# Mixture-of-experts stage of a Trainium2 kernel: gathers four slots ahead, and a second product whose distance shrinks from seven slots to two

## The chip, the cores and the metric

One NeuronCore of a Trainium2 chip. The metric is the device time of one execution in microseconds (us). The profile describes one execution, with the times of each instruction and transfer.

## What is computed

The input x has 4 sequences of 1024 tokens with 512 features. It is normalized by row (xn), and the output is the sum of three terms: x, causal attention with 16 heads and ALiBi biases on xn, and a mixture of 8 experts on xn, of which each token uses the best 2:

```
topw, sel = top_k(softmax(xn @ gate_w.T), 2); topw = topw / sum(topw)
gate_up = einsum('th,eoh->eto', xn, w1)          # 8 experts, 2*352 columns
g, u = split(gate_up, 2)
act = silu(g) * u
expert_out = einsum('eti,ehi->eth', act, w2)
out = einsum('eth,te->th', expert_out, combine)  # combine holds topw at sel
```

## The kernel before, in words

One function, `plan`, writes out the whole order of the work as a list of steps; each engine's function (`sync`, `tensor`, `vector`, `scalar`, `gpsimd`) walks through this one list and emits the steps that are its own, so the order within each engine is the order of the list. Steps of different engines meet through semaphores.

The first part (about 1180 us) computes normalization, attention, the routing and the split of the expert weights into pairs of fp16 numbers, which go to HBM and are read back at its end. Each normalized token row is kept in HBM as 1024 fp16 numbers (`xn_d`). The routing sorts the 8192 token-expert pairs by expert into NSLOT = 71 slots of 128 rows (`tl` holds the token numbers and weights of each slot). The output array already holds x plus attention when the experts begin.

The expert stage is one loop over slots. For a slot s the steps are:

- `gather` (POOL, L1664): an indirect DMA brings the 128 token rows of slot s (256 KB) into `xg`. There are XDEEP buffers; it waits for the transposition `mxt` of slot s - XDEEP.
- `mxt` (SP, L903): a transposing DMA from `xg` to `xT`, also XDEEP buffers. It waits for the gather of s and for the first product of slot s - XDEEP.
- `mgu` (PE, L1060): the first product, 24 matmuls into one of two PSUM buffers S (printed as "S").
- `msig`, `mglu`, `mah`, `mal` (ACT L1561, DVE L1434 and L1435, ACT L1569, DVE L1441): the gated activation, split in two fp16 parts.
- `mat`, `mac` (PE L1075, DVE L1449 and L1450): its six transpositions through PSUM (T) into `aTm`, which has AHEAD + 1 = 8 buffers.
- `mdn` (PE, L1091): the second product, 9 matmuls into PSUM O or M, in turn.
- `myo` (ACT, L1576): copies it, scaled by the row's weight, to `yo` in SBUF. Two buffers: it waits for the scatter of slot s - 2.
- `scatter` (POOL, L1675): an indirect DMA adds the 128 rows (256 KB) to the output in HBM. Different slots may hold the same token, so each scatter waits until the one before has landed.

In the loop (see `plan`) iteration s issues gather(s+2) and mxt(s+2), mgu(s), the transposition of slot s-1, the activation of slot s, and then mdn, myo and scatter of slot s-7 (AHEAD = 7). So on POOL's queue gather(s+2) stands right behind scatter(s-8), and on PE mdn(s-7) stands behind mgu(s). After the last first product, seven slots still have their second product and scatter to come. The semaphore waits of POOL's own list keep this order: a gather behind a waiting scatter waits too.

Of the kernel before, what the change touches and what calls it, by code (L numbers as in the profile page):

```python
# [8 lines left out]
P = 128  # L9
B, S, E = 4, 1024, 512  # L10
# [21 lines left out]
LAG = 4  # L32
J_ORDER = [0, 7, 1, 6, 2, 5, 3, 4]
AHEAD = 7
XDEEP = 3
ARENA = 50240
SLOPES = [2.0 ** (-0.5 * (h + 1)) for h in range(H)]
PASS = [(0, 0), (0, 1), (1, 0)]
# [97 lines left out]
def plan():  # L136
# [432 lines left out]
    def gather(s):  # L569
        add("gather", s, sem=f"xg{s % XDEEP}", inc=16)  # L570

# [14 lines left out]
    def turn_a(s):  # L586
# [2 lines left out]
        add("mac", s)  # L589
        o.leave("T", ("mat", s), ("mac", s))  # L590

    def down(s):
        o.take("Y", "mdn", s)
        add("mdn", s)
        add("myo", s)
        o.leave("Y", ("mdn", s), ("myo", s))
        add("scatter", s, inc=16)

    add("experts", inc=0)
    for s in range(XDEEP - 1):  # L600
        gather(s)
        turn_x(s)
    for s in range(NSLOT + AHEAD):
        if s + XDEEP - 1 < NSLOT:
            gather(s + XDEEP - 1)
            turn_x(s + XDEEP - 1)
        if s < NSLOT:
            up(s)
        if 1 <= s <= NSLOT:
            turn_a(s - 1)  # L610
        if s < NSLOT:
            gated(s)
        if s >= AHEAD:
            down(s - AHEAD)
    return o


# [18 lines left out]
def build(nc, ctx, T):  # L636
# [15 lines left out]
    def at(*step):  # L652

        name, value = o.count[step]
        return sems[name], value
# [84 lines left out]
    ac, to = place(to, [P, 2, I], F32)  # L740
    ah, to = place(to, [P, 2, 2, I], F16)
    aTm, to = place(to, [P, AHEAD + 1, 6, P], F16)
    yo, to = place(to, [P, 2, E], F32)
    assert to <= LATE, to

    GU = [ps(f"S{i}", [P, 1024], F32) for i in range(2)]
    SBK = [GU[0], GU[1][:, 0:512]]
# [705 lines left out]
    def scalar(act):  # L1453
# [4 lines left out]
        for step in o.steps:  # L1458
# [8 lines left out]
            elif kind == "xnd" and not key[0]:  # L1467
                b, half, i = key
                t = b * 8 + half * 4 + i
                on.wait_ge(*at("xnl", *key))  # L1470
                act.dma_start(xn_d[t * P:(t + 1) * P, :], XH[half_place(*key)]).then_inc(at(*step)[0], 16)
            elif kind == "xt" and key[3] == "a":
                b, half, i, _ = key
                tt = half * 4 + i
                tz = MBK[o.bank["xtp", b, half, i]][:, :].bitcast(F16)
                on.wait_ge(*at("xtp", b, half, i))
                if b:
                    on.wait_ge(*at("v", b - 1, NG - 1, 1, 3))
                act.activation(xnT[:, :, :, tt * P:(tt + 1) * P].rearrange("p a c n -> p (a c) n"),
                               tz.rearrange("p (c n) -> p c n", c=8), ACT.Copy).then_inc(sems["xta"], 1)  # L1480
            elif kind == "wqh":
                c, = key
                on.wait_ge(sems[f"w{c}"], 16)
                on.wait_ge(*at("scales", 0))
                act.activation(wqkv[:, 0, c, :], rawW[:, c, :], ACT.Copy, scale=col(SW)).then_inc(sems["wqh"], 1)
            elif kind == "gwh":
                on.wait_ge(sems["bias"], 32)
                on.wait_ge(*at("scales", 1))
                act.activation(gwh[:, 0, :, :].rearrange("p c n -> p (c n)"), gwf[:, :, :].rearrange("p c n -> p (c n)"),
                               ACT.Copy, scale=col(SG)).then_inc(sems["gwh"], 1)  # L1490
            elif kind == "woh":
                on.wait_ge(sems["w4"], 16)
                on.wait_ge(*at("scales", 2))
                act.activation(wo[:, 0, :, :].rearrange("p c n -> p (c n)"), rawA[:, 6144:8192], ACT.Copy,
                               scale=col(SWO)).then_inc(sems["woh"], 1)
            elif kind == "qk32":
                b, g, qk, half = key
                if (b, g, qk, half) != (0, 0, 0, 0):
                    n = 4 * (b * NG + g) + 2 * half + qk - 1
                    on.wait_ge(sems["qkl"], n + 1)  # L1500
                on.wait_ge(*at("qk", *key, 2))
                on.wait_ge(*at("scales", 1))
                cs, bs = (cq[:, g:g + 1], bq[:, g:g + 1]) if qk == 0 else (col(CK), bk[:, g:g + 1])
                act.activation(t32[:, 0, :], MBK[o.bank["qk", b, g, qk, half]][:, :], ACT.Identity, bias=bs,
                               scale=cs).then_inc(sems["qk32"], 1)
            elif kind == "exp":
                u, = key
                b, g, j, h, k, par = unit(u)
                w, r, m = P * (j + 1), u % 4, u % 8
                on.wait_ge(*at("mx", u))  # L1510
                if u >= 16:
                    on.wait_ge(*at("rx", u // 8 * 8 - 9))
                c = 4 * (1 - u % 2) + h
                act.activation(ring[r][:, 0:w], ring[r][:, 0:w], ACT.Exp, bias=mneg[:, m:m + 1], scale=-1.0,  # L1514
                               accum_out=rs[:, k, c:c + 1]).then_inc(sems["exp"], 1)
            elif kind == "pt" and key[2] == "a":
                u, i, _ = key
                k, h = unit(u)[4], unit(u)[3]
                c0, c1, to_, gap = turn_parts(u)[i]
                n = (c1 - c0) * P  # L1520
                on.wait_ge(*at("tr", u, i))
                if u >= 16:
                    on.wait_ge(*at("pv", u // 8 * 8 - 9))
                act.activation(PT[:, k, h, to_:to_ + gap * (c1 - c0 - 1) + 1:gap, :],  # L1524
                               TB[o.bank["tr", u, i]][:, 0:n].rearrange("p (c n) -> p c n", n=P),
                               ACT.Copy).then_inc(sems["pta"], 1)
            elif kind == "rsb":
                u, = key
                on.wait_ge(*at("rt", u))
                if u >= 8:  # L1530
                    on.wait_ge(*at("a32", u - 8))
                act.activation(Rsb[:, :], OB[:, 2 * P:4 * P], ACT.Copy).then_inc(sems["rsb"], 1)
            elif kind == "wsh":
                i, = key
                n, rows = w_rows(i)
                s = col(S1) if WCHUNK[i][1] < 4 else col(S2)
                on.wait_ge(*at("wload", "split", i))
                on.wait_ge(*at("wscale", 4))
                if i:
                    on.wait_ge(*at("wstore", i - 1))  # L1540
                else:
                    on.wait_ge(*at("xnd", 0, 1, 3))
                act.activation(hl[0:rows, 0, 0, 0:n], raw[0:rows, o.bank["wload", "split", i], 0:n], ACT.Copy,
                               scale=s[0:rows]).then_inc(sems["wsh"], 1)
            elif kind == "rex":
                on.wait_ge(*at("route", 0))
                act.activation(pr, pr, ACT.Exp).then_inc(sems["rex"], 1)
            elif kind == "experts":
                on.wait_ge(*at("pv", NU - 1))
                on.wait_ge(*at("rt", NU - 1))  # L1550
                on.wait_ge(*at("aT", NU - 1))
                for i in range(8):
                    on.wait_ge(*at("o", B - 1, i, 2))
                on.wait_ge(*at("listr"))
            elif kind == "msig":
                s, = key
                m = s % 2
                on.wait_ge(*at("mgu", s))
                if s >= 2:
                    on.wait_ge(*at("mal", s - 2))  # L1560
                act.activation(ex[:, m, :], GU[o.bank["mgu", s]][:, 0:I], ACT.Sigmoid,  # L1561
                               scale=col(I1)).then_inc(sems["msig"], 1)
            elif kind == "mah":
                s, = key
                m = s % 2
                on.wait_ge(*at("mglu", s))
                if s >= 2:
                    on.wait_ge(*at("mat", s - 2))
                act.activation(ah[:, m, 0, :], ac[:, m, :], ACT.Copy).then_inc(sems["mah"], 1)  # L1569
            elif kind == "myo":  # L1570
                s, = key
                m = s % 2
                on.wait_ge(*at("mdn", s))
                if s >= 2:
                    on.wait_ge(*at("scatter", s - 2))
                act.activation(yo[:, m, :], YB[o.bank["mdn", s]][:, :], ACT.Copy,  # L1576
                               scale=tl[:, s, 1:2].bitcast(F32)).then_inc(sems["myo"], 1)

    def gpsimd(pool):
# [10 lines left out]
        for step in o.steps:  # L1590
# [76 lines left out]
            elif kind == "scatter":  # L1667
# [4 lines left out]
                else:  # L1672
# [1 line left out]
                        on.wait_ge(*at("ostore", B - 1, i))  # L1674
                pool.indirect_dma_start(  # L1675
                    out=T["out"], out_offset=bass.IndirectOffsetOnAxis(tl[:, s, 0:1].bitcast(U32), 0),
                    in_=yo[:, s % 2, :], in_offset=None, compute_op=ALU.add).then_inc(sems["scatter"], 16)
        on.wait_ge(*at("scatter", NSLOT - 1))

    block = ctx.enter_context(nc.Block())  # L1680
# [74 lines left out]
```

## Time and profile before

| | us |
|---|---|
| median of 3 runs | 1713.99 |
| lowest, highest | 1702.82, 1714.74 |
| profiled execution, its time | 1701.79 |
| its span, first to last instruction | 1699.8 |

In the rows below times are us from the start of the span. PE is the matmul engine, PEld its weight loads, DVE, ACT and POOL the vector, scalar and GpSimd engines, SP the engine that issues most plain DMAs. "[1.67 <-X]" at the end of a timeline row is the engine's idle time just before it and what ended it. "issue" is time in which the engine waited for nothing that the profile shows. A DMA's "landing" is counted from the start of the instruction that issued it.

### The profile page before, as it was taken

The numbers are of one execution on the slowest core, as the hardware profiler recorded it, in microseconds if no ns is written. First come the engines' busy times: TensorE is split into PE (matmuls) and PEld (weight loads), VectorE is DVE, ScalarE is ACT, GpSimd is POOL, SyncE is SP. The second block draws the span as 40 slices with busy tenths as digits, with TensorE's granted clock in tenths as the row PEclk, the third lists the DMA queues.
The fourth block names the chain that finished last, engine by engine and source line by source line (L and its number), as shares of the span: only waits on it lengthen the run. The fifth ranks groups of instructions, "written<-read, shape, count | busy, mean of one in ns | idle before, by whom it ended". The sixth has DMA issues, their size and how long they took to land.

```text
span 1699.8 us, 35183 instructions
## 1 busy us (share of the span) xinstructions
PE 1472.6 (87%) x12629; PEld 875.3 (51%) x12629; DVE 1031.1 (61%) x2450; ACT 886.3 (52%) x2027; POOL 492.3 (29%) x576
## 2 busy tenths in 40 slices
PE   1699998998998899999899999995899998999882
PEld 1365564555555555555555555552555555555541
DVE  5478787675788777787788777772433333333320
ACT  3177776664777666776765577771222222222220
POOL 3111133121113212113311566411143343434322
PEclk9899999998999999999999999998899999999996
DMA  6153531333333254453133422545466666666653
GB/s 242 24 144 105 145 95 49 102 102 101 111 96 100 77 148 139 130 145 88 50 91 105 120 74 79 196 162 216 111 112 121 117 120 123 120 124 117 126 82 43
DMA packets 163460, 193.40 MB, mean 114 GB/s; under 512 B 88480, under 2 KB 104096, under 8 KB 163168
## 3 DMA queue, kind: packets, MB, share of 16 engines
q1 hardware_dynamic: 143760, 151.22, 32.3%
q0 software_dynamic: 17952, 37.30, 12.0%
q8 instruction: 109, 1.79, 0.4%
q10 hardware_dynamic: 1584, 2.64, 0.4%
q14 instruction: 55, 0.45, 0.1%
HBM read 93.45 MB, written 53.88 MB: 87 GB/s over the span
## 4 chain that ended last, share of the span: by engine, by line
PE 47%; DMA 16%; DVE 12%; issue 11%; ACT 6%; SPq 4%; POOL 3%; DVEq 0%; ACTq 0%; POOLq 0%
PE T L992 10%; PE S L1060 7%; PE O L1008 7%; DMA out<-arena,tl 6%; PE S L981 5%; PE M L949 4%; DMA arena<-arena 4%; PE S L949 4%; DMA arena<-xn_d,tl 4%; SPq L841 3%; DVE arena L1347 3%; PE M L1031 2%; ACT arena L1514 2%; ACT arena L1524 2%; PE S L966 2%
## 5 line engine op out<-in xcount | busy, mean ns | idle before, releaser
L1347 DVE CUSTOM_DVE_ANT_0 arena<-S,cF,nsl 128x1024 f32<-128x1024 f32 (+7 forms) x512 | 413.4, 811 | 58.5 <-PE S L981 54.5
L992 PE MATMUL T<-cF,arena 128*128 128x128 f32 x2304 | 366.9, 280 | 71.2 <-ACT arena L1524 37.4
L1514 ACT ACTIVATE arena<-arena,mneg 128x1024 f32<-128x1024 f32 (+7 forms) x512 | 395.3, 772 | 47.7 <-DVE mneg L1347 46.8
L1524 ACT ACTIVATE arena<-T 128x512 f32<-128x512 f32 (+3 forms) x543 | 241.6, 458 | 247.2 <-PE T L992 243.1
L992 PEld LDWEIGHTS T<-cF,arena 128*128 128x128 f32 x2304 | 266.8, 142 | 173.0 <-ACT arena L1524 44.6
L1060 PE MATMUL S<-arena 128*128 x1704 | 274.0, 319 | 59.4 <-issue 30.6
L1060 PEld LDWEIGHTS S<-arena 128*128 128x128 f16 x1704 | 168.6, 99 | 167.1 <-issue 77.4
L1358 DVE COPY arena<-T 128x512 f32<-128x512 f32 (+3 forms) x289 | 153.8, 535 | 130.2 <-PE T L992 128.4
L1008 PE MATMUL O<-arena 128*32 128x128 f32 (+1 forms) x3328 | 210.9, 329 | 9.0 <-DVE arena L1378 7.7
L981 PE MATMUL S<-arena 96*128 96x512 f16 (+3 forms) x768 | 211.9, 330 | 4.6 <-DVE mneg L1347 3.0
L1675 POOL DMA_INDIRECT out<-arena,tl x71 | 111.9, 1577 | 281.0 <-ACT arena L1576 194.7
L1449 DVE COPY arena<-T 128x512 f16<-128x512 f16 x71 | 30.1, 424 | 249.7 <-PE T L1075 249.7
L1561 ACT ACTIVATE arena<-S,sc 128x352 f32<-128x352 f32 x71 | 39.3, 553 | 227.5 <-PE S L1060 227.5
L1621 POOL TENSOR_TENSOR arena<-arena 128x512 f16<-128x512 f32 x64 | 74.2, 1159 | 271.8 <-DVE arena L1328 264.7
L1008 PEld LDWEIGHTS O<-arena 128*32 128x32 f32 x3328 | 67.3, 109 | 130.0 <-issue 114.0
L1631 POOL CAST arena<-arena 128x256 f16<-128x256 f32 x64 | 27.4, 428 | 308.8 <-DVE arena L1378 308.8
L949 PE MATMUL M<-arena 128*128 128x512 f16 x384 | 99.3, 387 | 14.6 <-DVE arena L1272 14.6
L1514 ACT ACTIVATION_READ_ACCUMULATOR arena<-arena,mneg 128x1 f32 x512 | 99.9, 195 | 0.0
L949 PE MATMUL S<-arena 128*128 128x512 f16 x384 | 99.0, 386 | 0.0
L1569 ACT ACTIVATE arena<-arena 128x352 f16<-128x352 f32 x71 | 35.2, 496 | 110.4 <-DVE arena L1435 110.4
L1664 POOL DMA_INDIRECT arena<-xn_d,tl x71 | 69.8, 983 | 62.7 <-DMA arena<-arena 41.3
L1638 POOL TENSOR_TENSOR arena<-arena 128x512 f32<-128x512 f32 x32 | 40.4, 1275 | 162.3 <-DMA arena<-in_x 162.3
(168 smaller groups left out, 1810.1 us busy)
## 6 DMA issues: line engine op xcount, KB each, us to landing
arena<-arena SPq DMA_DIRECT2D x192, 128.0 KB, 2.4
arena<-in_w1T SPq DMA_DIRECT2D x64, 352.0 KB
arena<-in_x SPq DMA_DIRECT2D x64, 256.0 KB, 3.6
w_d<-arena SPq DMA_DIRECT2D x32, 352.0 KB
arena<-w_d SPq DMA_DIRECT2D x16, 704.0 KB, 10.1
arena<-in_w2T SPq DMA_DIRECT2D x32, 256.0 KB
out<-arena SPq DMA_DIRECT2D x32, 256.0 KB, 2.2
xn_d<-arena SPq DMA_DIRECT2D x24, 256.0 KB, 2.0
```

Source lines behind the costliest of these rows:

```text
L949: tp = pe.matmul(z[:, :], wqkv[:, w_, c, f:f + P], xnT[:, a, c, half * 512:half * 512 + 512], start=(third == 0 and c == 0), stop=(third = ...
L981: tp = pe.matmul(z[:, n0:n1], stk[par][0:96, h, 0, j * P:(j + 1) * P], stk[par][0:96, h, 1, n0:n1], start=True, stop=True)
L992: tp = pe.transpose(z[:, (c - c0) * P:(c - c0 + 1) * P], ring[u % 4][:, c * P:(c + 1) * P], idf)
L1008: tp = pe.matmul(OB[32 * x:32 * x + 32, f:f + n], V[par][:, kt, x * D:(x + 1) * D], flat[:, x, c * P:c * P + n], start=(kt == 0), stop=(kt ...
L1060: tp = pe.matmul(y[:, i * 512:i * 512 + I], xT[:, s % XDEEP, 4 * a + c, :], weights[:, bass.ds(reg[s] + (w_ * NX * W1N + c * 2 * I + i * I ...
L1347: dve.tensor_tensor_reduce(ring[r][:, 0:w], SBK[o.bank["score", u]][:, 0:w], rel[:, S - w:S], nsl[:, hh:hh + 1], 3.0e38, ALU.add, ALU.min, ...
L1358: dve.tensor_copy(PT[:, k, h, to_:to_ + gap * (c1_ - c0_ - 1) + 1:gap, :], TB[o.bank["tr", u, i]][:, 0:n].rearrange("p (c n) -> p c n", n= ...
L1514: act.activation(ring[r][:, 0:w], ring[r][:, 0:w], ACT.Exp, bias=mneg[:, m:m + 1], scale=-1.0, accum_out=rs[:, k, c:c + 1]).then_inc(sems[ ...
L1524: act.activation(PT[:, k, h, to_:to_ + gap * (c1 - c0 - 1) + 1:gap, :], TB[o.bank["tr", u, i]][:, 0:n].rearrange("p (c n) -> p c n", n=P), ...
L1621: pool.tensor_tensor(st[:, 2 * qk + 1, lo:hi], t32[:, 0, :], st[:, 2 * qk, lo:hi], ALU.subtract).then_inc(sems["qkl"], 1)
L1664: pool.indirect_dma_start(out=xg[:, s % XDEEP, :], out_offset=None, in_=xn_d, in_offset=bass.IndirectOffsetOnAxis(tl[:, s, 0:1].bitcast(U3 ...
L1675: pool.indirect_dma_start(out=T["out"], out_offset=bass.IndirectOffsetOnAxis(tl[:, s, 0:1].bitcast(U32), 0), in_=yo[:, s % 2, :], in_offse ...
```

## The change

XDEEP becomes 4: gathers are issued four slots ahead and token transpositions three slots ahead, each with four buffers. YDEEP = 4 gives `yo` four buffers instead of two; it now lies where the weights of the attention's output projection were. The distance between mgu and mdn is a function of the slot: 7 up to s = 24, then one less every 11 slots (6 from s = 25, 5 from 36, 4 from 47, 3 from 58, 2 from 69). Where it gets smaller, one iteration carries two second products with their scatters.

```diff
-XDEEP = 3
+XDEEP = 4
+YDEEP = 4
@@
+    done = [0]
+    def behind(s):
+        return max(2, AHEAD - max(0, s - 14) // 11)
@@
     add("experts", inc=0)
+    for s in range(XDEEP):
+        gather(s)
     for s in range(XDEEP - 1):
-        gather(s)
         turn_x(s)
     for s in range(NSLOT + AHEAD):
+        if s + XDEEP < NSLOT:
+            gather(s + XDEEP)
         if s + XDEEP - 1 < NSLOT:
-            gather(s + XDEEP - 1)
             turn_x(s + XDEEP - 1)
         if s < NSLOT:
             up(s)
@@
-        if s >= AHEAD:
-            down(s - AHEAD)
+        while done[0] <= min(s - behind(s), NSLOT - 1):
+            down(done[0])
+            done[0] += 1
@@
-    yo, to = place(to, [P, 2, E], F32)
-    assert to <= LATE, to
+    assert to <= LATE, (to, LATE)
+    yo, to = place(LATE, [P, YDEEP, E], F32)
@@ scalar, myo
-                if s >= 2:
-                    on.wait_ge(*at("scatter", s - 2))
-                act.activation(yo[:, m, :], YB[o.bank["mdn", s]][:, :], ACT.Copy,
+                if s >= YDEEP:
+                    on.wait_ge(*at("scatter", s - YDEEP))
+                act.activation(yo[:, s % YDEEP, :], YB[o.bank["mdn", s]][:, :], ACT.Copy,
@@ gpsimd, scatter
-                    in_=yo[:, s % 2, :], in_offset=None, compute_op=ALU.add).then_inc(sems["scatter"], 16)
+                    in_=yo[:, s % YDEEP, :], in_offset=None, compute_op=ALU.add).then_inc(sems["scatter"], 16)
```

## Rows read from the trace of the kernel before

**Rows 1.** The page's head: span and busy time by engine

```profile
span 1699.8 us, 35183 instructions
PE 1472.6 (87%) x12629; PEld 875.3 (51%) x12629; DVE 1031.1 (61%) x2450; ACT 886.3 (52%) x2027; POOL 492.3 (29%) x576
```

**Rows 2.** Busy time by stretch: us, engines, clock, DMA share, GB/s

```profile
1200.00:1250.00 50.00, 48.26 (x339) 30.72 (x337) 23.49 (x53) 14.63 (x27) 11.54 (x10) 1.00 0.50 98
1232.00:1636.00 404.00, 369.40 (x2395) 218.97 (x2393) 135.85 (x306) 99.67 (x184) 157.66 (x123) 0.99 0.67 119
1643.00:1700.00 57.00, 25.49 (x104) 10.84 (x102) 2.84 (x7) 6.43 (x10) 12.43 (x8) 0.71 0.33 42
```

**Rows 3.** Timeline of PE in the expert stage: start, us, engine, line

```profile
1235.16 0.50 PE L1075 MATMUL T<-idh,arena 128*128 128x128 f16 x6
1235.49 2.12 PE L1091 MATMUL M<-arena 128*128 x9
1237.45 3.74 PE L1060 MATMUL S<-arena 128*128 x24
1241.03 0.50 PE L1075 MATMUL T<-idh,arena 128*128 128x128 f16 x6
...
1251.15 3.75 PE L1060 MATMUL S<-arena 128*128 x24 [1.67 <-DMA arena<-arena]
```

**Rows 4.** Chain that ended last, 1237 to 1258: start, us, what

```profile
1237.86 0.68 ACT arena L1576
1238.81 1.57 POOL out L1675
1240.68 4.36 DMA arena<-xn_d,tl
1245.06 5.21 DMA arena<-arena
1250.26 0.89 issue
1251.15 3.75 PE S L1060 x24
...
1257.44 0.68 ACT arena L1576
1258.38 1.58 POOL out L1675
```

**Rows 5.** Waits, 1232 to 1636: total us, times, longest

```profile
POOL out L1675 <- ACT arena L1576: 181.7, 47, 12.5
...
POOL out L1675 <- DMA out<-arena,tl: 57.7, 15, 5.0
...
PE S L1060 <- DMA arena<-arena: 26.2, 19, 2.0
```

**Rows 6.** The scatter's line L1675, 1233 to 1636

```profile
L1675 POOL DMA_INDIRECT out<-arena,tl x62: 1569/1583/1637, 1232.8 to 1635.0; - x62
...
DMA to landing us min/median/max: 4.6/5.5/7.0
```

**Rows 7.** The scatter's line L1675, 1650 to 1700

```profile
L1675 POOL DMA_INDIRECT out<-arena,tl x8: 1552/1554/1555, 1651.1 to 1690.6; - x8
...
DMA to landing us min/median/max: 4.7/4.8/5.1
```

**Rows 8.** Timeline of POOL, 1373 to 1387

```profile
1373.16 1.57 POOL L1675 DMA_INDIRECT out<-arena,tl  x1 [4.22 <-DMA out<-arena,tl]
1375.04 0.99 POOL L1664 DMA_INDIRECT arena<-xn_d,tl  x1 [0.30 <-issue]
1379.03 1.58 POOL L1675 DMA_INDIRECT out<-arena,tl  x1 [3.00 <-DMA out<-arena,tl]
1380.92 0.99 POOL L1664 DMA_INDIRECT arena<-xn_d,tl  x1 [0.30 <-issue]
1385.67 1.57 POOL L1675 DMA_INDIRECT out<-arena,tl  x1 [3.77 <-DMA out<-arena,tl]
```

**Rows 9.** The tail's chain: one scatter to the next

```profile
1679.41 4.84 DMA out<-arena,tl
1684.29 0.71 issue
1685.00 4.84 DMA out<-arena,tl
```

More of the change, by code:

```diff
@@ L1571, in scalar @@
                 s, = key
-                m = s % 2
                 on.wait_ge(*at("mdn", s))
-                if s >= 2:
-                    on.wait_ge(*at("scatter", s - 2))
-                act.activation(yo[:, m, :], YB[o.bank["mdn", s]][:, :], ACT.Copy,
+                if s >= YDEEP:
+                    on.wait_ge(*at("scatter", s - YDEEP))
+                act.activation(yo[:, s % YDEEP, :], YB[o.bank["mdn", s]][:, :], ACT.Copy,
                                scale=tl[:, s, 1:2].bitcast(F32)).then_inc(sems["myo"], 1)
```

## The prediction, on record before the changed kernel ran

> **What bounds the kernel now.** The page's head comes first: PE is busy 87% of the span [rows 1], but that is a mean over different stages and the change touches only the last 500 us. So the second view is the busy time by stretch [rows 2]. While first products run without second ones (1200 to 1250, mostly), PE is busy 48.3 of 50 us. From 1232 to 1636, where each iteration has both, it is busy 369.4 of 404 us (91%) at a granted clock of 0.99, and the DMA engines 67%. In the tail, from 1643 on, PE is busy 25.5 of 57 us. The third view is the timeline of PE [rows 3]: an undisturbed iteration takes 1241.03 - 1235.16 = 5.87 us from one activation transposition to the next, and a disturbed one has its first product waiting 1.67 us for a token transposition. There are 19 such waits in the stretch, 26.2 us [rows 5].
>
> The actual pace is read at the scatters: the first starts at 1232.8 and the 62nd at 1635.0 [rows 6], so 402.2 / 61 = 6.59 us per slot, 0.72 more than PE needs. The chain of waits tells why [rows 4]: scatter at 1238.81, gather behind it at 1240.68, landed at 1245.04, transposition landed at 1250.27, first product at 1251.15, then the second product behind it on PE, its copy at 1257.44, the next scatter of the same chain at 1258.38. That is 19.57 us. In slots: scatter(k) is followed on POOL by gather(k+10); after mgu(k+10) PE runs mdn(k+3), which feeds scatter(k+3). So the ring turns three slots in 19.57 us, 6.52 per slot, which is the 6.59 measured. **The bound is the latency of this ring**, not an engine.
>
> Right behind it stands a second bound. Scatters are serial: each waits for the landing of the one before. In the tail, beside no gather or transposition, they land in 4.8 us [rows 7] and follow each other every 5.6 us (4.84 landing plus 0.71 of issue [rows 9]); the eight of them go from 1651.1 to 1690.6, 39.5 / 7 = 5.64 each. Beside the other transfers the median landing is 5.5 us, the longest 7.0 [rows 6]. In 15 of the 62 cases it is already the scatter's own landing that released the next one, and in 47 the copy on ACT [rows 5].
>
> **The change part by part.**
> *Gathers four ahead, transpositions three.* No transfer or instruction is added; 71 gathers and 71 transpositions stay. On POOL, gather(s+4) now stands behind scatter(s-8), so scatter(k) is followed by gather(k+12), and behind mgu(k+12) comes mdn(k+5). The same 19.57 us now carry five slots: 3.9 per slot. The ring is off the path. With the shorter distance it stays so (at distance 2 scatter(k) is followed by gather(k+7), and behind mgu(k+7) again comes mdn(k+5)). The gather's wait on mxt(s) doesn't bind, since mgu(s), just ahead, needs the same; the transposition's wait on mgu(s-1) leaves three iterations of 5.87 us for some 6 us of work (5.21 + 0.89, [rows 4]). At the start one more gather is issued beside the weight loads. I take nothing for it; the bound is below one gather's landing, 4.4 us late, if PE's first product waited for it, and -1 us.
>
> *What is late next.* PE needs 5.87 per slot, the scatter chain its landing plus 0.7. The price of the contended scatter decides everything, and no row shows it in the new regime, so I bound it. Lower end: 5.87, where PE binds, since the scatter alone would do 5.64. Upper end: the periods in which the landing did release the next scatter, 57.7 / 15 = 3.85 us of idle time [rows 5] plus 1.58 scatter, 0.30 and 0.99 gather [rows 6, 8], = 6.72. This is biased upward, since a scatter becomes the bound just when it was slow. The median landing gives 5.5 + 0.7 = 6.2 to 6.25. Where scatters in a row were bound by landing, as at 1373.16, 1379.03 and 1385.67 [rows 8], periods of 5.87 and 6.64 follow each other, mean 6.25; a few landings near 7.0 lift that. The order on the DMA engines in the new regime is the one of these rows (gather 1.9 us behind the scatter, transposition when the gather has landed), so I take 6.35, near the median row rather than the selected one.
>
> *The sum.* Scatter 0 starts as before at 1232.8: distance and first iterations are unchanged. Of the 70 periods to scatter 70, 59 carry a gather (12 to 70) and 11 don't (before: 61 and 9). 59 x 6.35 = 374.7, 11 x 5.64 = 62.0, together 436.7, against 1690.6 - 1232.8 = 457.8 now. After the last scatter's start come 9.2 us in both. The saving is 21.1 us.
>
> *Distance from seven to two.* It moves five second products (about 2 us each, [rows 3]) from behind the last first product to before it. In the kernel before that would shorten the tail of serial scatters, 5.64 each. Here I price it at nothing by itself: the scatters are late against PE anyway, and moving PE's work doesn't move them. The cover is PE's slack: 59 x (6.35 - 5.87) = 28 us against 5 x 2 us of moved work. If that cover were gone (scatters at PE's pace) the moved work would be hidden in part, and the tail shorter by up to 5 x 5.64 = 28 us against what seven pending slots would take.
>
> *Four buffers for the copy.* Before, `myo` waits for scatter(s-2), and behind it on ACT stand the next sigmoid and cast, for which DVE and PE wait in turn. With four it can only wait less. In the stretch ACT's copies are not seen waiting except in the tail, so it is worth 0 to 3 us, and I take 0. With two scatters in one iteration (five times) it keeps the second one's copy from blocking ACT.
>
> A rule to weigh. The trace shows 4.8 us for a lone scatter of 256 KB and 5.5 us beside other traffic [rows 6, 7]. The Trainium skill, page "DMA: Bandwidth & Descriptors", section "Anatomy of one DMA — SWDGE (gpsimd) path", has a fit of about 2.0 us plus bytes / 436e3, which would be 2.6 us here. By that estimate the scatter chain would take about 3.3 us a slot, PE would bind at once, and the kernel would land on the first rival's time. The traces stand against it, even for the lone scatter.
>
> **The rivals.**
> *PE becomes the bound.* If contended scatters come down to 5.1 us of landing or less, the pace is PE's 5.87: 59 x 5.87 + 62.0 = 408.3, 49.5 us saved, 1664.5. For it: after a longer pause scatters land in 4.6 to 5.1, the low end of [rows 6]. Against it: packed closer, they land later. 0.13.
> *No gain.* The scatter chain paces at the selected 6.72: 59 x 6.72 + 62.0 = 458.5, +0.7 us, 1714.7. For it: the 15 waits already there. Against: their selection. 0.15.
> *Slower.* Gathers and transpositions, now free of the ring, lie beside every scatter on the same DMA engines (67% busy already, [rows 2]), and its landing moves to halfway between median and longest, 6.25 us: a period of 7.0, 59 x 7.0 + 62.0 = 475.0, +17.2 us, 1731.2. It decides from a mean period of (457.8 - 62.0) / 59 = 6.71. The ring before left pauses in which a scatter ran alone; without them there are none. Against: the number of bytes and the order are the same. 0.10.
>
> **How the numbers follow.** The forecast case has 0.62. The profiled execution took 1701.8 (its span and 2.0 around it), 12 us less than the median of 1714.0; the three runs are 1702.8, 1714.0 and 1714.7. I apply the saving to the median: 1714.0 - 21.1 = 1692.9 (an execution like the profiled one would come to 1680.7). Its own range is a period of 6.2 to 6.5, 1684 to 1702. A measurement of this kernel can tell about 1% from no change, 17 us, which needs a period below 6.42; of the forecast case I give that 0.7. Faster by over 1%: 0.62 x 0.7 + 0.13 = 0.56. Slower by over 1%: 0.09. Within 1%: 0.35. The range takes in PE's bound below and the no-gain case above: 1664 to 1716.
>
> **What would show it.** Right: PE's waits for token transpositions are not on the path, or are there without cost; nearly all scatters in the middle are released by the landing of the one before (now 15 of 62); 6.2 to 6.5 us between scatters; ACT's copies wait for scatters in the middle too; the first scatter still near 1233; 9 us behind the last scatter's start. Wrong: the scatters are mostly released by ACT's copy (then PE or a ring binds), or the median landing leaves 5.4 to 5.8, or the first product starts late. If the number of scatters behind the last first product falls to three and the tail after it gets shorter by several 5.64 us, the distance was worth more than I give it.

## The result, and the profile after

| | before | changed |
|---|---|---|
| median, us | 1710.97 (4 runs) | 1685.73 (4 runs) |
| lowest, highest | 1702.82, 1714.74 | 1681.75, 1689.71 |
| profiled execution, its time and span | 1701.79, 1699.8 | 1683.42, 1681.5 |

The ratio is 0.9859, with a 95% interval of 0.9811 to 0.9907. A second comparison beside the experiments gave 0.990 (0.9862 to 0.9938). The prediction was 1692.9 against a median of 1714.0, which is a ratio of 0.9877; for an execution like the profiled one it gave 1680.7, and 1683.4 came. The medians moved by 25.2 us and the two profiled executions by 18.4. The four executions of the kernel before spread over 12 us, and only one of them has a trace, so where that spread lies isn't known.

The busy time by stretch and the waits of the changed kernel from 1232 to 1636 answer to [rows 2] and [rows 5]:

```profile
1232.00:1636.00 404.00, 379.83 (x2445) 225.42 (x2444) 136.12 (x308) 103.05 (x189) 162.27 (x123) 0.97 0.67 119
```

```profile
POOL out L1684 <- DMA out<-arena,tl: 186.4, 54, 5.5
POOL out L1684 <- ACT arena L1585: 40.3, 9, 11.4
...
PE S L1070 <- DMA arena<-arena: 16.7, 4, 6.0
...
ACT arena L1585 <- DMA out<-arena,tl: 0.7, 1, 0.7
```

These rows show a bound change hands. Of the 64 scatters that start there, 54 are released by the landing of the one before, where it was 15 of 62; PE's waits for token transpositions fell from 19 (26.2 us) to 4 (16.7 us). The scatter's own line, to set beside [rows 6]:

```profile
L1684 POOL DMA_INDIRECT out<-arena,tl x64: 1562/1569/1827, 1232.7 to 1632.3; - x64
...
DMA to landing us min/median/max: 4.6/5.5/7.2
```

The first scatter stands where it stood, the landing is the same 5.5 us, and 63 periods take 399.6 us, 6.34 each, where 61 took 6.59 each before. In the kernel before, the same 63 periods took 418.3 us (1232.8 to 1651.1), and the last of them was by far the longest, 10.14 us. It is the last turn of the ring, here in the chain that ended last:

```profile
1629.06 1.58 POOL out L1675
...
1630.94 6.34 DMA arena<-xn_d,tl
...
1637.30 3.95 DMA arena<-arena
1641.25 0.97 issue
1642.21 5.43 PE S L1060 x24
...
1651.12 5.06 DMA out<-arena,tl
```

The last gather took 6.34 us to land, and the last first product took 5.43 us at a granted clock of 0.68. In the changed kernel the period at that place is 6.4 us. So some 4 of the 18.3 us that the stage lost come from this one turn.

The timeline of POOL shows the new rhythm, with each scatter here waiting for the last one's landing:

```profile
1461.81 1.57 POOL L1684 DMA_INDIRECT out<-arena,tl  x1 [3.12 <-DMA out<-arena,tl]
1463.68 1.01 POOL L1673 DMA_INDIRECT arena<-xn_d,tl  x1 [0.30 <-issue]
1467.95 1.56 POOL L1684 DMA_INDIRECT out<-arena,tl  x1 [3.25 <-DMA out<-arena,tl]
```

In the expert stage the chain that ended last is now mostly scatters (19% of the whole span, 6% before). Gathers and transpositions, 8% before, are no longer among its larger lines.

```profile
PE 45%; DMA 22%; issue 11%; DVE 11%; ACT 6%; SPq 3%; POOL 2%; POOLq 0%; DVEq 0%; ACTq 0%
DMA out<-arena,tl 19%; PE T L1002 11%; PE O L1018 7%; PE S L991 5%; PE M L959 4%; PE S L959 4%; PE S L1070 4%; DVE arena L1357 3%; SPq L851 3%; PE M L1041 2%; ACT arena L1524 2%; PE S L976 2%; ACT arena L1534 2%; DVE arena L1368 1%; PE M L976 1%
```

### The profile page after: what moved, and what is told of

Its sections match the earlier page's. It is cut to its first block, busy times and chain, and to the rows that moved or that the text cites. A ratio compares the mean times of both kernels' runs of the same rounds, so it can differ in the third digit from the quotient of the medians.

```text
span 1681.5 us, 35180 instructions
## 1 busy us (share of the span) xinstructions
PE 1464.8 (87%) x12629; PEld 874.1 (52%) x12629; DVE 1032.1 (61%) x2450; ACT 886.9 (53%) x2027; POOL 496.0 (29%) x576
## 4 chain that ended last, share of the span: by engine, by line
PE 45%; DMA 22%; issue 11%; DVE 11%; ACT 6%; SPq 3%; POOL 2%; POOLq 0%; DVEq 0%; ACTq 0%
DMA out<-arena,tl 19%; PE T L1002 11%; PE O L1018 7%; PE S L991 5%; PE M L959 4%; PE S L959 4%; PE S L1070 4%; DVE arena L1357 3%; SPq L851 3%; PE M L1041 2%; ACT arena L1524 2%; PE S L976 2%; ACT arena L1534 2%; DVE arena L1368 1%; PE M L976 1%
```

## The experiments

The experiments ran on two chips; whether the first comparison ran on one of them isn't known. In the experiments the kernel before has a median of 1734 to 1739 us. The profiled executions there spend 26 to 32 us more ahead of the experts (the first product starts between 1220 and 1226 in all but one, instead of 1194). So each run is read by its ratio to the kernel before on its own chip, and by its expert stage, here the time from the first to the last scatter's start: 457.8 before, 439.5 changed. The stage is read from one execution of each kernel, and the kernel before was traced only in the first comparison. So a difference of a few us in the stage proves nothing unless the ratio agrees.

**The distance held at seven**

```diff
-        return max(2, AHEAD - max(0, s - 14) // 11)
+        return AHEAD
```

> The change with the distance held at seven throughout (four gathers, four copy buffers stay). Theory (the serial chain of scatters binds, so where PE's second products stand doesn't matter): first scatter near 1233, 70 periods of about 6.28 us as in the changed kernel, span 1678 to 1686, ratio to the kernel before 0.984 to 0.990. Rival (the shorter distance carries part of the gain by moving second products ahead of the last first product): the span is 10 to 20 us longer than the changed kernel's, 1692 to 1702.

Ratio 0.9883 (0.9854 to 0.9912), scatters from 1257.6 to 1698.8, 441.3 us. The theory held: with gathers four ahead, the shorter distance adds nothing that can be measured. It does move work: with distance seven, 11 scatters start behind the start of the last first product, with the shrinking distance 6 (5 when the changed kernel ran again). The stage is as long all the same.

**Distance, or so it was meant**

```diff
-XDEEP = 4
-YDEEP = 4
+XDEEP = 3
+YDEEP = 2
```

> Only the shrinking distance, with three gather buffers, gathers two ahead and two copy buffers as before. Theory (the ring scatter, gather, transposition, first product, second product still binds at 19.6 us for three slots): median period between scatters stays near 6.5 to 6.6, and the shorter tail is paid for by ring pace: ratio to the kernel before 0.997 to 1.004. Rival (distance alone shortens the tail): five scatters of 5.64 us gone from the tail, 15 to 28 us faster, ratio 0.984 to 0.991.

Ratio 0.9865 (0.9827 to 0.9903), stage 434.5 us: the whole gain, and the rival seemed right. But the edit wasn't what the text says. In the changed kernel's loop the gather is XDEEP ahead and the transposition XDEEP - 1; with XDEEP = 3 the gather is three slots ahead, where the kernel before had two. Two later runs take it apart. (The profiled execution, 1706.2 us, is 6 us below this run's median, about as much as its stage is below 440.)

**Two copy buffers**

```diff
-YDEEP = 4
+YDEEP = 2
```

> The change with two buffers for the scaled copy of the second product instead of four. Theory: the scatter chain binds and the copy only has to be ready one scatter ahead: 0 to 3 us more than the changed kernel, ratio to the kernel before 0.984 to 0.990, with copies on ACT now waiting for scatters. Rival (a blocked copy holds the sigmoid and cast behind it on ACT, and so PE, until scatters starve): 8 us or more, ratio over 0.991.

Ratio 0.9879 (0.9849 to 0.9908), stage 439.6 us. The waits of this run from 1232 to 1636:

```profile
POOL out L1684 <- DMA out<-arena,tl: 160.5, 46, 4.8
ACT arena L1585 <- DMA out<-arena,tl: 159.5, 49, 5.9
```

The copies now wait 160 us in all for scatters and it costs nothing that can be measured (0.9883 with four buffers and distance seven, 0.990 for the changed kernel again). This fits the theory: the scatter that they wait for is the one that binds anyway.

**Distance two from the first slot**

```diff
-        return max(2, AHEAD - max(0, s - 14) // 11)
+        return 2
```

> The change with distance two from the first slot. Theory (the serial chain of scatters binds, so the whole stage moves with its first scatter): the first scatter starts near 1213 instead of 1232.7, the 70 periods take 440 to 444 us, span 1662 to 1668, ratio to the kernel before 0.973 to 0.979. Rival (the seven slots are a cushion: without them PE's stalls reach the scatters): periods of 6.5 us and more, span 1675 or longer.

Ratio 0.9767 (0.9733 to 0.9801), median 1696.7 against 1713.7 for distance seven on the same chip: 17 us less. The timelines of PE and POOL in this run:

```profile
1229.59 9.71 PE L1070 MATMUL S<-arena 128*128 x48 [22.43 <-issue]
...
1244.79 0.50 PE L1085 MATMUL T<-idh,arena 128*128 128x128 f16 x6
1245.12 1.68 PE L1101 MATMUL O<-arena 128*128 x7
```

```profile
1248.44 1.64 POOL L1684 DMA_INDIRECT out<-arena,tl  x1 [16.83 <-ACT arena L1585]
```

The first scatter starts 18.9 us behind the first product, 38.5 us in the changed kernel (1194.17, 1232.66). The stage takes 444.0 us from there, and the last scatter starts 462.9 us behind the first product instead of 478.0. The start moved 20 us and the end 15. (This execution began its experts 3 to 10 us later than the others of the experiments, so its absolute times are late.)

**The changed kernel again**

> The changed kernel once more, beside the others on one chip. Ratio to the kernel before as found, 0.981 to 0.991; first to last scatter 437 to 443 us, 6.2 to 6.4 us each while gathers run.

Ratio 0.990 (0.9862 to 0.9938), stage 440.7 us.

**Two chains of scatters**

```diff
-        add("scatter", s, inc=16)
+        add("scatter", s, sem=f"scatter{s % 2}", inc=16)
...
+    out2_d = dram("out2_d", [(NT + 1) * P, E], F32)
...
-                if s:
-                    on.wait_ge(*at("scatter", s - 1))
-                else:
+                if s > 1:
+                    on.wait_ge(*at("scatter", s - 2))
+                elif s == 0:
...
-                    out=T["out"], ...
+                    out=(out2_d if s % 2 else T["out"]), ...
```

> The changed kernel with the scatters of odd slots going to a second array, so that a scatter waits only for the one two before; the second array is left out of the output. Theory (the serial chain of scatters binds): the pace falls to PE's 5.87 us per slot, PE's second product of the last slot ends about 45 us earlier, and the span is 35 to 50 us shorter than the changed kernel's; ratio to the kernel before 0.957 to 0.967, scatters released by the copy on ACT. Rival (the DMA engines as a whole bind, the chain only shows it): landings stretch beyond 7 us and the span falls by less than 15 us, ratio over 0.976.

Ratio 0.9588 (0.9532 to 0.9643). Busy time of this run from 1330 to 1600, and POOL's timeline:

```profile
1330.00:1600.00 270.00, 270.00 (x1780) 162.20 (x1779) 99.60 (x225) 75.60 (x139) 121.02 (x94) 1.00 0.83 136
```

```profile
1400.97 1.57 POOL L1685 DMA_INDIRECT out<-arena,tl  x1 [2.99 <-ACT arena L1586]
1402.85 1.02 POOL L1674 DMA_INDIRECT arena<-xn_d,tl  x1 [0.30 <-issue]
1406.84 1.56 POOL L1685 DMA_INDIRECT out_d<-arena,tl  x1 [2.98 <-ACT arena L1586]
```

The output lacks the sums of the odd slots, since the second array is left out of it. PE is busy 270.00 of 270 us, the pace is its 5.87 per iteration (in each block of 11 iterations the shrinking distance lets 12 scatters through, 5.5 us each), 63 of the 71 scatters are released by ACT's copy and only 3 by a landing, and the stage takes 385.4 us. With the chain split PE is what is left, and the DMA engines are busy 83% without binding. (The rival was to show itself by landings beyond 7 us; the profile gives no landings for this run, but the span fell by 51 us, where the rival allowed less than 15.) So the serial wait is the bound of the changed kernel, and the next one, PE, stands 55 us of stage below it.

**Without gathers, and without transpositions**

```diff
-        if s + XDEEP < NSLOT:
+        if s + XDEEP < 12:
             gather(s + XDEEP)
...
```

```diff
-        if s + XDEEP - 1 < NSLOT:
+        if s + XDEEP - 1 < 12:
             turn_x(s + XDEEP - 1)
...
```

The lines not shown drop or replace the semaphore waits for steps that no longer exist.

> The changed kernel with the gathers of slots 12 to 70 left out (old rows are transposed again). It prices the gather's share of a contended scatter. Theory (a scatter beside other transfers lands later, 5.5 against 4.8 us): median landing 5.0 to 5.2 us, pace 5.87, set by PE, span 22 to 30 us shorter than the changed kernel's, ratio 0.969 to 0.975. Rival (gathers don't disturb scatters, transpositions do): landing stays at 5.4 to 5.5 and the span within 6 us, ratio 0.982 to 0.990.

> The changed kernel with the token transpositions of slots 12 to 70 left out (the first product uses old ones). It prices the transposition's share. Theory: median landing 5.0 to 5.2 us, pace 5.87, span 22 to 30 us shorter than the changed kernel's, ratio 0.969 to 0.975. Rival (transpositions don't disturb scatters, gathers do): landing 5.4 to 5.5, span within 6 us, ratio 0.982 to 0.990.

Ratios 0.971 (0.9648 to 0.9771) and 0.967 (0.9615 to 0.9725). The landing of a scatter from 1330 to 1600, in the changed kernel, without gathers, and without transpositions:

```profile
DMA to landing us min/median/max: 4.7/5.5/7.2
```

```profile
DMA to landing us min/median/max: 4.7/5.0/5.6
```

```profile
DMA to landing us min/median/max: 4.7/4.9/5.8
```

Without the gathers a scatter lands 0.5 us earlier, without the transpositions 0.6, and the stage falls from 440 to 411 and to 401 us. The two don't add up: a scatter beside neither lands in 4.8 [rows 7], so taking one away brings nearly all of it. The first run stayed within its forecast of the ratio. The second gained more than forecast: the ratio was to be 0.969 to 0.975 and the landing 5.0 to 5.2. Nor does PE alone set the pace, as both expected. From 1330 to 1600 PE is busy 270.00 of 270 us in both, but 40 of 46 scatters and 32 of 47 are still released by the landing before. The two limits lie close together here. The Trainium skill, page "DMA: Bandwidth & Descriptors", section "Issuing engines are not separate DMA queues", says that transfers started by different engines run on the same 16 DMA engines and interleave. The runs agree: transpositions come from SP's queue and slow a scatter from POOL's by about as much as POOL's own gathers do.

**One gather buffer less than before**

```diff
-XDEEP = 3
+XDEEP = 2
```

> The kernel before with XDEEP = 2 (gather and transposition one slot ahead). Ring theory: scatter(k) is followed by gather(k+9), and behind mgu(k+9) stands mdn(k+2), so two slots share the 19.6 us: 9.8 us per slot over some 62 slots against 6.6, about 190 to 205 us slower, ratio 1.11 to 1.12. Rival (the gather's lead only has to cover its own landing and transposition, about 10 us, and costs what it misses): one slot ahead is 5.9 us, so 4 us missed per slot at most, and less with overlap: under 100 us, ratio below 1.06.

Ratio 1.1258 (1.1194 to 1.1323), even a little over the ring theory's figure and far from the rival's. One turn of the chain of waits in this run:

```profile
1402.73 1.60 POOL out L1675
1404.33 0.30 issue
1404.64 4.05 DMA arena<-xn_d,tl
...
1408.71 4.39 DMA arena<-arena
1413.10 0.90 issue
1414.01 6.06 PE S L1060 x24
...
1422.61 0.68 ACT arena L1576
1423.29 0.27 issue
1423.56 1.58 POOL out L1675
```

That is [rows 4] again, 20.8 us for two slots; over the 62 periods with a gather the mean is 10.3 us per slot. The turn is longer than 19.57 because of the first product, 6.06 us instead of 3.75, while gather and transposition were somewhat shorter. PE's granted clock was 0.61 during this product. Over the stretch from 1330 to 1600, where PE is busy 183 of 270 us, it was 0.83 in the mean.

```profile
1330.00:1600.00 270.00, 183.02 (x1014) 102.67 (x1014) 57.70 (x130) 42.26 (x78) 67.17 (x53) 0.83 0.43 77
```

**Only the gather moved up by one slot** (distance seven, three and two buffers)

```diff
-XDEEP = 4
-YDEEP = 4
+XDEEP = 3
+YDEEP = 2
...
-        return max(2, AHEAD - max(0, s - 14) // 11)
+        return AHEAD
```

> Distance seven throughout, three gather buffers and two copy buffers as in the kernel before; only the gather moves up by one slot in the list (three ahead, transpositions still two ahead). This one edit was also in the run called distance only, so that run was not what its text said. Ring theory: scatter(k) is followed by gather(k+11), behind mgu(k+11) stands mdn(k+4), so four slots share 19.6 us, 4.9 per slot, and the scatter chain binds as in the changed kernel: ratio 0.983 to 0.991. Rival (deeper buffers are what helps): ratio 0.995 or more.

Ratio 0.9896 (0.9854 to 0.9938), stage 440.0 us. One step moved in the list, no buffer added, and the gain is there. With the next run this also settles the second one: its gain was the gather's.

**The distance alone** (in the kernel before)

```diff
...
-        if s >= AHEAD:
-            down(s - AHEAD)
+        while done[0] <= min(s - behind(s), NSLOT - 1):
+            down(done[0])
+            done[0] += 1
```

> The kernel before with the shrinking distance alone: gathers and transpositions two ahead, three and two buffers. Theory A (each of the five steps of the distance gives the ring one slot more, so 12 scatters come out of 11 turns of 6.52 us, 5.98 each, below the chain's 6.3): the first 17 periods stay at 6.5 to 6.7, later ones fall to 6.2 to 6.4, ratio 0.986 to 0.993. Theory B (as the prediction had it, the distance by itself is worth nothing): 6.5 to 6.6 throughout, ratio 0.997 to 1.004.

Ratio 1.002 (0.9988 to 1.0051): theory B. Only 4 scatters start behind the start of the last first product, where the kernel before has 8, and nothing was gained by it. The profiled execution doesn't fit as well: its stage is 450.4 us, 7.4 below the kernel before. But it was the fastest of 12 (1723.8 against a median of 1735.5), and no trace of the kernel before was kept on this chip to set beside it. The verdict rests on the ratio, which leaves no room for theory A's 0.986 to 0.993. POOL's timeline at a step of the distance shows what theory A left out:

```profile
1375.02 0.99 POOL L1670 DMA_INDIRECT arena<-xn_d,tl  x1 [0.30 <-issue]
1379.02 1.58 POOL L1681 DMA_INDIRECT out<-arena,tl  x1 [3.00 <-ACT arena L1582]
1384.53 1.58 POOL L1681 DMA_INDIRECT out<-arena,tl  x1 [3.93 <-DMA out<-arena,tl]
1386.41 1.03 POOL L1670 DMA_INDIRECT arena<-xn_d,tl  x1 [0.30 <-issue]
```

Two scatters stand ahead of the next gather, so it comes 11.4 us after the last one (11.8 to 13.3 at the three other steps that had a gather to hold up). By this reading the ring gets one slot more and one scatter's wait more; no run tests that by itself.

**Distance two, few buffers** (gathers three ahead)

```diff
-XDEEP = 4
-YDEEP = 4
+XDEEP = 3
+YDEEP = 2
...
-        return max(2, AHEAD - max(0, s - 14) // 11)
+        return 2
```

> Distance two from the first slot with three gather buffers (gathers three ahead, transpositions two) and two copy buffers. Theory (only the first scatter's start and the serial chain count): as the run with distance two from the start, ratio 0.973 to 0.980. Rival (with short distances the extra buffers are a needed cushion): ratio 0.983 or more.

Ratio 0.980 (0.9766 to 0.9833), median 1698.2. The first scatter comes 17.9 us behind the first product (1222.4, 1240.3). The point lies at the theory's end and below the rival's, whose 0.983 is just in the interval; this run and the one with more buffers overlap. Both beat the changed kernel as it ran beside the experiments, 0.990 (0.9862 to 0.9938).

## Why the prediction was right, point by point

*The ring.* Right, and shown three times: take a slot away and the kernel is 12.6% slower along the same chain; move only the gather by one slot and the gain appears; go to four ahead and nothing more comes (441.3 against 440.0 us of stage). The prediction's 19.57 us for three slots became two slots in 20.8 where one was removed. Of its signs, "nearly all scatters released by the landing" came out as 54 of 64.

*What is late next.* Right. The price of a contended period was the argument's weakest number: 6.35 taken between 5.87 and 6.72, since no row showed it. To come within 0.02 us was partly luck. It measured 6.33 (the 63 periods to 1632.3 took 399.6 us; four of them, without a gather, took 26.4 in sum, the other 59 373.3). Choosing the median landing over the selected waits was the right choice: a wait is recorded only where the scatter was slow, so a mean over waits overstates it.

*The sum.* 436.7 us forecast, 439.5 measured. The difference of 2.8 comes from one term: the four scatters that follow a scatter with no gather between (7.27, 7.11, 6.01 and 5.99 us) were priced at the tail's 5.64. Their landings (5.7, 6.4, 5.3 and 5.2 us) are those of contended scatters, and a transposition of an earlier gather is issued within 0.8 us of each of the four; the first waited 0.9 us beyond its landing and the usual 0.7, for a reason that the profile doesn't show. The 59 others give back 1.4 of it, and the last seven, 39.8 us, are 0.4 over. So errors of both signs are in the sum. It forecast 21.1 us saved; the profiled pair saved 18.3 in the stage and the medians 25.2 in all, one below and one above.

*The distance.* Right in its price, nothing: alone 1.002, and held at seven beside the other edits 0.9883 against 0.9859 and 0.990. Its remark that in the kernel before the shorter distance would shorten the tail wasn't borne out as a gain: 4 scatters were left behind the last first product instead of 8, and the time stayed. In the changed kernel 6 are left, not the three that the prediction named as a sign against itself, and 11 with distance seven. The prediction looked for its worth at the end of the stage and didn't ask what a short distance does at its start, where it is the wait for the first scatter. In the change the first steps keep seven, so nothing was missed in the forecast, but 15 to 17 us were left there.

*Four copy buffers.* Right in size (nothing), wrong in the sign expected: copies were to be seen waiting for scatters in the middle. With four buffers one waits in that stretch, 0.7 us; with two, 49 do. The likely reason, not tested by itself, is that PE never gets four slots ahead of the scatters, since each gather still stands behind a scatter on POOL.

*The rivals.* No gain and slower are out by the ratio's interval and by the landing, which stayed at 5.5. PE as the bound, at 1664.5, was a true neighbour: it is what splitting the chain gives (the profiled spans of the changed kernel and of the two chains on one chip are 1710.4 and 1659.2, 51.2 us apart). The Trainium skill's fit for one transfer, an estimate of 2.6 us by the page "DMA: Bandwidth & Descriptors", section "Anatomy of one DMA — SWDGE (gpsimd) path", would have put the kernel there without any edit of the chain. No scatter whose landing a profile gives landed in under 4.5 us, even without gathers or transpositions.

## What to carry to other kernels

When every engine is busy in tenths and none is full, count the slots of a ring: time once around it, divided by how many items it carries, and compare that with the engine and with every serial chain; the largest is the pace, and lifting one bound only exposes the next. Where transfers are serial by necessity, the stage ends when the first of them starts plus their number, so start the first one early; a software pipeline's depth ahead of such a chain is paid for at its beginning (here the start moved 20 us and the end 15). And check what an experiment's edit does to the order of the list, not only to its constants.

## What was not expected of the hardware

A serial scatter of 256 KB with addition costs 5.5 us of landing beside gathers and transpositions, 4.9 to 5.0 beside one of them and 4.8 alone. The 5.5 came at DMA engines busy only 67%: here landing grew well before they were full. At 83% busy, with two chains, only 3 of 71 scatters waited for a landing. And the same kernels took 23 to 31 us more in the experiments than in the first comparison, with an expert stage of the same length (439.5 and 440.7 us for the changed kernel). What makes the part ahead of the experts longer there is not shown.
